# Fourier layer of a fused four-block image kernel: the next item's transposes ahead of the mode mixing, weights and MLP constants prepared elsewhere

## What is computed

```
fty = rfft(x along columns)[..., :16];  f1 = einsum('bixy,ioy->boxy', fty, w1)
ftx = rfft(x along rows)[:, :16];       f2 = einsum('bixy,iox->boxy', ftx, w2)
h   = irfft(f1) + irfft(f2)
y   = layer_norm(relu(h @ ff_w0 + ff_b0) @ ff_w1 + ff_b1)
```

## Time and profile before

| what | value |
|---|---|
| median of 3 runs | 5486.84 us (5483.71 to 5490.64) |
| profiled execution: its own time | 5499.24 us |
| profiled execution: span | 5497.5 us |
| busy over the span: TensorE matmul, weight load | 86%, 63% |
| busy over the span: DVE, ACT, POOL | 64%, 54%, 37% |
| DMA over the span | 822.69 MB, mean 150 GB/s |
| granted TensorE clock, mean | 0.933 |

### The profile page before, as it was taken

The page is one execution under the profiler, slowest core; times in us unless marked ns, Lnnn a source line. Parts: engine busy times, 40 slices in busy tenths (PEclk is TensorE's granted clock), DMA queues, the critical chain, the costliest instruction groups (busy, mean ns, idle before and its releaser), DMA issues. The chain is left out here.

```text
span 5497.5 us, 111057 instructions
## 1 busy us (share of the span) xinstructions
PE 4738.3 (86%) x37534; PEld 3483.8 (63%) x37534; DVE 3512.8 (64%) x10149; ACT 2975.6 (54%) x6431; POOL 2060.1 (37%) x1516
## 2 busy tenths in 40 slices
PE   6999999999999997469999899974666569999982
PEld 5777777777777775146776677721222348988882
DVE  6778888888888786125666566612899513555554
ACT  1888888888888881123333333332555423555552
POOL 1666666666666660022332233301556300222221
PEclk8999999999999999699999999997999759999995
DMA  7222222222222229742221222255888539999982
GB/s 275 71 71 71 70 71 71 71 71 71 71 71 71 71 60 314 291 139 71 68 68 59 91 67 69 66 183 169 246 272 275 180 123 345 328 325 330 333 260 57
DMA packets 844717, 822.69 MB, mean 150 GB/s; under 512 B 65224, under 2 KB 705665, under 8 KB 835329
## 3 DMA queue, kind: packets, MB, share of 16 engines
q1 hardware_dynamic: 834386, 796.65, 46.5%
q10 hardware_dynamic: 6720, 10.76, 0.6%
q0 software_dynamic: 3072, 8.39, 0.4%
HBM read 607.88 MB, written 207.68 MB: 148 GB/s over the span
## 5 line engine op out<-in xcount | busy, mean ns | idle before, releaser
L299 POOL TENSOR_TENSOR at_bias<-at_tri,at_mask 128x1024 f32<-128x1024 f32 x512 | 1205.1, 2377 | 751.2 <-DVE at_neg_max L460 740.2
L409 ACT ACTIVATE at_probs<-at_neg_s,at_neg_max 128x256 f32<-128x256 f32 x2048 | 894.8, 502 | 0.1
L460 DVE CUSTOM_DVE_ANT_0 at_neg_s<-at_p_s,at_bias 128x256 f32<-128x256 f32 x2048 | 744.1, 420 | 47.1 <-PE at_p_s L333 47.1
L344 PE MATMUL at_p_t<-all_ident,at_probs 128*128 128x128 f32 x4096 | 628.6, 276 | 0.3 <-ACT at_probs_t L401 0.2
L1721 PE MATMUL dw_p_conv<-dw_xw,dw_wts 128*128 128x128 f32 x4096 | 512.9, 278 | 114.9 <-DMA dw_wts<-patch_w 58.5
L344 PEld LDWEIGHTS at_p_t<-all_ident,at_probs 128*128 128x128 f32 x4096 | 484.3, 141 | 136.8 <-issue 85.1
L1721 PEld LDWEIGHTS dw_p_conv<-dw_xw,dw_wts 128*128 128x128 f32 x4096 | 484.5, 192 | 131.6 <-issue 129.5
L921 ACT ACTIVATE ml_h<-ml_p,l_b 128x512 f32<-128x512 f32 x384 | 263.9, 687 | 556.3 <-PE ml_p L880 556.3
L1822 POOL TENSOR_TENSOR dw_xr<-dw_xr,all_b_plain 128x512 f32<-128x512 f32 x128 | 188.1, 1469 | 880.2 <-DMA dw_xr<-x3t 880.2
L468 DVE COPY at_probs_t<-at_p_t 128x512 f32<-128x512 f32 x512 | 352.6, 689 | 205.0 <-PE at_p_t L344 205.0
L889 PE MATMUL ml_p<-l_w1s,ml_h 128*128 128x128 f32 x4096 | 478.4, 275 | 0.8 <-issue 0.8
(11 more groups left out here) (210 smaller groups left out, 9353.4 us busy)
## 6 DMA issues: line engine op xcount, KB each, us to landing
dw_wts<-patch_w SPq DMA_DIRECT2D x256, 512.0 KB, 8.1
dw_xw<-planes SPq DMA_DIRECT2D x128, 528.0 KB, 6.1
sp_xs<-x SPq DMA_DIRECT2D x128, 512.0 KB, 9.9
planes<-pw_plane SPq DMA_DIRECT2D x128, 264.0 KB, 4.5
in_xs<-in_x_dram SPq DMA_DIRECT2D x32, 1024.0 KB, 7.7
at_xs<-in_x_dram SPq DMA_DIRECT2D x256, 128.0 KB, 2.4
at_kvs<-in_L_conv_kv_x_dram SPq DMA_DIRECT2D x256, 128.0 KB, 2.5
at_mask<-in_L_conv_mask_bias_dram SPq DMA_DIRECT2D x256, 128.0 KB, 3.3
```

Source lines behind the costliest of these rows:

```text
L299: pool.tensor_tensor(bias[:, n % 2, part], tri[:, part], mask[:, n % 4].unsqueeze(1).broadcast_to((128, 4, COLS)), ALU.add).then_inc(maske ...
L344: mm = pe.transpose(p_t[h % 2][:, kh, qh * 128:(qh + 1) * 128], probs[:, h, qh, kh * 128:(kh + 1) * 128], ident[:, :])
L409: e = act.activation(probs[:, h, qh, :], neg_s[:, n % 2, h, qh, :], ACT.Exp, bias=neg_max[:, n % 2, i:i + 1], scale=-1.0)
L460: t = dve.tensor_tensor_reduce(neg_s[:, n % 2, h, qh, :], p_s[h][:, qh, :], bias[:, n % 2, i, :], -1.0, 3.0e38, ALU.add, ALU.min, neg_max[ ...
```

## The change

- `spectra` gets the weights. POOL loads `w` (both axes) at the start of that stage, from its own DMA queue, and DVE arranges `wcat` after its last statistics instruction. `w` and `wcat` are now allocated around both stages.
- In the mixing stage TensorE's list is `turn(0)`, then for every n `turn(n+1)`, `mix(n)`. So that nothing is overwritten, ACT now also waits for mixing n-2 before it writes `ft` again.
- `fs` has four buffers in place of two, and `gs` three in place of two. Loops with a register are written out with constants.
- The six loads of MLP constants are issued by ACT at the start of the mixing stage, ahead of its table load. DVE's preparation of them is put behind its copies of items 5, 6 and 7. The stage `prepare_mlp` is gone.

The diff, cut to its core:

```diff
@@ spectra
+        @block.gpsimd
+        def _(pool):
+            for axis in range(2):
+                pool.dma_start(w[:, axis], weights[axis]).then_inc(w_loaded, 16)
...
                 st.then_inc(summed, 1)
             dve.wait_ge(w_loaded, 32)
             for axis in range(2):
                 by_mode = w[:, axis].rearrange("p o k z -> p z k o")
                 dve.tensor_scalar(wcat[:, axis, :, 0, :], by_mode[:, 1], -1.0, None, ALU.mult)
...
@@ mix_modes -> mix_modes_and_prepare_mlp
-        fs = m.sb("fs", [128, 2, 2, HALVES, CH])
+        fs = m.sb("fs", [128, depth, 2, HALVES, CH])
-        gs = m.sb("gs", [128, 2, HALVES, 2, CH])
+        gs = m.sb("gs", [128, 3, HALVES, 2, CH])
...
+            for n in range(count):
+                src = spec[n // MODES].rearrange("(k z) (h p) c -> k p z h c", z=2, p=128)[n % MODES]
+                if n >= depth:
+                    sp.wait_ge(turned, n - depth + 1)
+                for z in range(2):
+                    sp.dma_start(fs[:, n % depth, z], src[:, z]).then_inc(loaded[n % depth], 16)
...
+            turn(0)
+            for n in range(count):
+                if n + 1 < count:
+                    turn(n + 1)
+                mix(n)
...
+            act.dma_start(w0[:, :], ff_w0).then_inc(ff_loaded, 16)
...
+            for n in range(count):
+                act.wait_ge(turned, n + 1)
+                if n >= 2:
+                    act.wait_ge(made, n - 1)
...
+                dve.tensor_copy(gs[:, n % 3], p_mix[n % 2][:, :, :, :]).then_inc(read, 1)
+                if n == 5:
+                    dve.wait_ge(ff_loaded, 16 * 6)
+                    dve.tensor_reduce(rows[:, :], w1s[:, :, :], mybir.AxisListType.X, ALU.add)
...
@@ fourier_layer
-        prepare_mlp(nc, ff_w0, ff_b0, ff_w1, ff_b1, ln_g, ln_b, w0, w1s, rows, b0, vec_rows, eps[:, :])
```

More of the change, by code:

```diff
@@ L519, with spectra @@
 LN_EPS = 1e-5
-def spectra(nc, x1, forward, ident, stats, spec):
+def spectra(nc, x1, forward, ident, stats, spec, weights, w, wcat):
     quads, group, rows = ROWS // 16, 4, 4
@@ L618, in _ @@
                 st.then_inc(summed, 1)
[L621 to L628, removed]
-        fs = m.sb("fs", [128, 2, 2, HALVES, CH])
-        ft = m.sb("ft", [128, 2, 2, COLS])
-        gs = m.sb("gs", [128, 2, HALVES, 2, CH])
[L632 to L719, removed]
@@ L723, in _ @@
                 dve.tensor_scalar(wcat[:, axis, :, 0, :], by_mode[:, 1], -1.0, None, ALU.mult)
-                dve.tensor_copy(wcat[:, axis, :, 1, :], by_mode[:, 0]).then_inc(w_split, 1)
-                dve.tensor_copy(wcat[:, axis, :, 2, :], by_mode[:, 1]).then_inc(w_split, 1)
-            def item(axis, k, p, use, n):
-                dve.wait_ge(made, n + 1)
-                if not (isinstance(n, int) and n < 2):
-                    dve.wait_ge(stored[p], use * 32)
-                dve.tensor_copy(gs[:, p], p_mix[p][:, :, :, :]).then_inc(read, 1)
@@ L1035, in fourier_layer @@
     with ExitStack() as ctx:
[L1036 to L1040, removed]
         m = Scope(nc, ctx, "l1")
@@ L1047, in fourier_layer @@
         b0 = m.sb("b0", [128, HIDDEN // 128])
-        prepare_mlp(nc, ff_w0, ff_b0, ff_w1, ff_b1, ln_g, ln_b, w0, w1s, rows, b0, vec_rows, eps[:, :])
+        with nc.sbuf_tensor("l1_w", [128, 2, CH, MODES, 2], fp) as w, \
+                nc.sbuf_tensor("l1_wcat", [128, 2, MODES, 3, CH], fp) as wcat:
+            with nc.sbuf_tensor("l1_stats", [128, TOKENS // BANK, 6], fp) as stats:
+                spectra(nc, x1, consts["forward"], ident, stats, spec, (w1, w2), w, wcat)
+                group_norm_coefficients(nc, "l1", stats[:, :, :].rearrange("p a b -> p (a b)"), group_mean,
+                                        coef[:, 0:1], coef[:, 1:2])
+            mix_modes_and_prepare_mlp(nc, spec, wcat, ident, coef[:, 0:1], coef[:, 1:2], mixed, ff_w0, ff_b0, ff_w1, ff_b1,
+                                      ln_g, ln_b, w0, w1s, rows, b0, vec_rows, eps[:, :])
         waves = m.sb("waves", [128, COLS, ROWS // 2])
@@ L1053, in fourier_layer @@
             mlp(nc, half, x1, mixed[0], consts["inverse_cols"], waves, prepared, ident, x2, stats_out)
[L1056 to L1071, removed]
-                sp.dma_start(vec_rows[:, i, :], v.rearrange("(a c) -> a c", a=1).to_broadcast((128, CH))).then_inc(loaded, 16)
-        @block.vector
-        def _(dve):
-            dve.memset(eps, LN_EPS)
-            dve.wait_ge(loaded, 16 * 6)
-            dve.tensor_reduce(rows[:, :], w1s[:, :, :], mybir.AxisListType.X, ALU.add)
-            dve.tensor_reduce(mean[:, :], vec_rows[:, 0, :], mybir.AxisListType.X, ALU.add).then_inc(step, 1)
-            dve.wait_ge(step, 1)
-            dve.tensor_scalar(rows[:, :], rows[:, :], 1.0 / CH, None, ALU.mult)
-            dve.tensor_scalar(mean[:, :], mean[:, :], 1.0 / CH, None, ALU.mult).then_inc(step, 1)
-            dve.wait_ge(step, 2)
-            for b in range(blocks):
-                dve.tensor_scalar(w1s[:, b, :], w1s[:, b, :], rows[:, b:b + 1], None, ALU.subtract)
-            dve.tensor_scalar(vec_rows[:, 0, :], vec_rows[:, 0, :], mean[:, :], None, ALU.subtract)
 TAPS = 9
```

80 lines of the change are left out of this document (78 added, 2 removed).

## The result

| what | before | after |
|---|---|---|
| median of 4 runs each | 5488.74 us (5483.71 to 5494.23) | 5443.09 us (5440.93 to 5450.81) |
| ratio, with its 95% interval | | 0.9919 (0.9902 to 0.9936) |
| profiled execution: its own time | 5499.24 us | 5442.86 us |
| mean granted TensorE clock | 0.933 | 0.936 |

The change makes the kernel 45.7 us faster, where 48.9 was forecast. The time of 5443.1 us lies 5 us above the predicted 5438 and inside the range.

A forecast was written before the change was run, and what follows sets the result against it. Mixing was taken as bound by latency in a closed TensorE, ACT, TensorE chain. Mixing -49.4, prepare_mlp -9.5 and weights in spectra +10 gave -48.9 us, off the 5486.84 median: 5438 us, range 5428 to 5454.

The forecast's parts named there:

- Period of an item: Mixing stage: with the next transposes ahead of the mixing, an item takes 2.25 us (2.1 to 2.6) instead of 3.46.
- The three waits: Mixing stage: waits now standing between blocks of TensorE's work, whose price the forecast said isn't seen.
- The rival of a POOL backlog (A): Mixing: POOL clears about 1.7 us behind every store, so the period stays at 3.4 us, time 5474; chance 0.07.
- The half-way period (C): Mixing: period of 2.6 to 3.0 us from gaps at waits or 512-byte loads, time 5449 to 5461; chance 0.12.
- The third is worth nothing: Mixing's store buffers: one is free after 4.0 us, so two would have done as well as three.
- Start of the stage: Mixing stage: first mixing starts at 5.75 us, last ends at 80.0 instead of 129.4; gain 49.4 us including the period.
- End of the stage: Mixing's end: copy, stores, last wait and POOL drain of 5.28 us stay; change 0, bounds -2 to +3 us.
- prepare_mlp: Stage after mixing: removed, its 2.2 us of DVE work spread over items 5, 6 and 7; gain 9.5 us.
- Weights in spectra: Spectra: loading 4.19 MB of mode weights takes its time from the tiles; loss 10 us, bounds 6 to 12.
- there is no room: Spectra's first half: tiles need 356 GB/s against 364 measured, so the weight load takes its time from the tiles.
- no later part makes up: Spectra: the second group's modes stand 8.5 us late, and that delay is never recovered.
- Rival B: Spectra: weights cost only 0 to 4 us, as DVE and TensorE pace first-half tiles; time 5428 to 5432; chance 0.12.

## Why the prediction was right, and where it was not

**Period of an item: right.** 2.25 us was forecast with bounds of 2.1 to 2.6, and 2.17 was measured. It is the sum of 1.60 and 0.57 us of weight loads with nothing between, the lower end of the argument ("if the 0.03 us gaps close"). The three waits cost nothing. Undoing the order alone brought the period to 3.36 and cost 36.0 us, near the 31 x 1.21 = 37.5 of the forecast. The rival of a POOL backlog (A) is out: POOL waits for DVE in each item, and the drain stands only at the end. The half-way period (C) did not come.

**"The third is worth nothing": nearly so, by a sum that was too short.** With two buffers of each kind the stage was 3.0 us longer, but only some 0.4 us of it are the third `gs`. The sum took one landing of 1.5 us behind the end of the issue, read at the quiet end of the stage. In the changed kernel's mixing the median landing is 2.8 us from a store's issue, and up to 4.5. The second store of an item is issued 0.53 us behind the first, so the buffer is free after 0.69 + 0.30 + 0.53 + 2.8 = 4.3 us and not 4.0. Two buffers give 2 x 2.17 = 4.3, which is why DVE waits in 14 items; three give 6.5. What the prediction did not price is the depth of `fs`: a load lands 2.6 us after its issue in the middle and up to 3.4, where 2.2 was taken, and with two buffers three loads came late and cost 1.5 us.

**Start of the stage: right in sum by two errors.** The last mixing ends 79.1 us after the stage's first issue; 80.0 was forecast. The first mixing was to start at 5.75 us and started at 9.5. The step that failed took `turn(0)` and then `mix(0)`, though the new list has `turn(1)` between, and gave the second item's loads the usual landing of 2.2 us where they took up to 7.1. The old order started at 6.65. What made up for these 3.8 us was the shorter period (31 x 0.08 = 2.5 us) and the time at the lower clock. From the first mixing to the second, 3.2 + 1.5 + 0.6 = 5.3 us were put down, and it was 3.3 us. That part is luck: the same stretch took 3.3 to 4.3 us in the nine profiles with the new order, and in two of these the next item was late by another 0.5 us.

**End of the stage: right.** 9.9 us from the last mixing's end to the next stage's first issue, against 10.2 before. The drain of 5.28 us stayed. The runs add what it is tied to: stores from SP's queue end with a drain of 7 ns, and the stage is 6.5 us shorter.

**prepare_mlp: right.** 9.5 us forecast, 9.6 measured as a stage. Its DVE work lies in the mixing with no wait of TensorE to show for it.

**Weights in spectra: the price was right, the total was not.** The load costs 10.7 us at the fast rate (217.8 against 207.1) and 10.8 us at the slow one (222.9 against 212.1), where I took 10. But spectra grew by only 5.8 us. The step that failed is the one that took the DMA rate as given: "there is no room", 356 against 364 GB/s. The allocation of `w` and `wcat` and the MLP's tensors ahead of the ring moved it by chance onto a better address, which took 5.1 us off. That is also why "no later part makes up" was wrong. Counted from the stage's first issue, the first tile was 10.1 us late, all sixteen groups of the first half 9.6 us, and the last modes of the stage 6.0 us: with 385 GB/s against a need of 356 the ring filled again, and the second half made up 3.6 us. Rival B gave 0 to 4 us for another reason, a pace set by TensorE and DVE. That pace is real, a group every 6.62 us in all kernels, but it doesn't hide the load, since it leaves the late groups no way to catch up; at the old rate the whole 10.8 us appear.

The Trainium skill's page "Perfetto Trace Analysis" (Roofline) says that about 358 GB/s is a core's share when both cores of a pair use the memory, and that a single core can draw up to some 435. I had cited only the share. The trace agrees with the higher figure: 406 GB/s over 60 us of spectra's second half, and 426 before.

**The sum.** By stages, the change gave -54.6 us where -48.9 was forecast. Of the 5.7 us between, 4.2 are spectra's. The median difference is 45.7, and the 8.9 us to the stages' sum are of the size of the untouched stages' scatter (23 us in the depthwise stage alone). The forecast time is only 5 us off because spectra's lucky address and this scatter partly cancel; that is partly luck.

## What to carry to other kernels

When TensorE waits in each item for the engine that feeds its second product, put the next item's first product ahead. Here the period became the sum of TensorE's own weight loads, and it could be read off the old timeline to 0.1 us. Then look at what the new list puts ahead of the very first item.

Choose a buffer count by the landing time under the new traffic, not by one landing in a quiet moment, and ask of a wait whether TensorE ever waits behind it: here 14 waits of DVE cost 0.4 us, and three late loads 1.5 us. Where a stage fills the DMA engines, write down the address of its ring: here a 32-byte tensor allocated ahead of it cost 3 to 6% of the rate, and a change that allocates anything else will move it.

A load of megabytes belongs in a stage whose DMA share is low (attention, 0.26: nothing), not in one that is full (10.7 us). Look for a drain at the end of a stage whose stores POOL issues: here it was 5.28 us, and gone when SP issued them.

## What the runs showed of the hardware that was not expected

- Same transfers, same DMA share, different rate by the ring's address: 363 to 385 GB/s (6%) in the first half of spectra, 395 to 406 (3%) in the second. The DMA view of the kernel before, from 2096 to 2120 and from 2210 to 2270 us, gives packets and MB of SP's queue in the two:

```profile
q1 hardware_dynamic: 7697, 7.65, 96.4%
...
q1 hardware_dynamic: 10910, 21.04, 93.3%
```

  These are pieces of about 1 KB and 2 KB. Twice the piece and half the loss point to a cost for each piece. Estimated from these rates over 16 engines it is 2 to 3 ns (1024 x 16 / 363 GB/s = 45.1 ns against 42.6; 2048 x 16 / 395 = 83.0 against 80.7).
- POOL's sequencer drains for 5.28 us at the end of the mixing, in which it issued 64 stores, after its last wait for their data is over; SP's takes 7 ns in the same place. The 5.28 us are no fixed price. In the mlp stages, where POOL only computes, its drain takes 1.36 us. In spectra of the changed kernel it begins behind POOL's two issues and lasts until the weights have landed, 13.0 us after the second issue at 2080.4; there it is hidden. This is the line view of L530.

```profile
L530 POOLq DRAIN  x1: 13411/13411/13411, 2080.2 to 2080.2; - x1
```

- The depthwise stage, at some 307 GB/s and a DMA share of 0.99 to 1.00, took 879 to 902 us with the same code. What makes it scatter stays open. By the sizes of what is allocated ahead of them its tensors too start off a multiple of 256 bytes, and moving them onto one was not tried.
